# New merge strings for the four step streams of a conv, attention and Fourier kernel

## The chip, the cores and the metric

The kernel runs on one core of a Trainium2 chip. Its metric is the device time of one execution in microseconds. Five engines work side by side, each on its own instructions in order: PE (TensorE, matmuls), DVE (VectorE), ACT (ScalarE), POOL (GpSimd) and SP (SyncE, which here issues all DMAs). They wait for each other on semaphores only.

## What is computed

32 images of 56 x 56 pixels and 24 channels, in f32, go through six residual blocks:

```python
# twice: conditional convolution block, all weights mixed per image
rw = sigmoid(mean(x, (1, 2)) @ Wr + br)                   # 4 experts
h = relu(bn(conv1x1(x, mix(rw, Wpw)) + rw @ bpw))         # 24 -> 96
h = relu(bn(depthwise3x3(h, mix(rw, Wdw)) + ...))
x = x + bn(conv1x1(h, mix(rw, Wpwl)) + rw @ bpwl)         # 96 -> 24
t = tokens(x)                                             # 3136 x 24
t = t + linear_attention(layernorm(t))                    # 6 heads, no softmax
t = t + ffn_fp8(layernorm(t))                             # 24 -> 96 -> 24, rounded to fp8
u = layernorm(t)                                          # Fourier attention over the tokens
X = fft(relu(bn(u @ w1.T)), axis=tokens)
y = real(ifft(relu(X.real * r - X.imag * i + rb) + 1j * relu(X.imag * r + X.real * i + ib)))
t = t + bn(y @ w2.T)
t = t + ffn_fp8(layernorm(t))
```

## The kernel before

The images go in 8 quads of 4. The 4 x 24 channels of a quad lie on partitions, the 3136 tokens on the free axis, in seven chunks of 448. Quads are worked in four streams of steps, and each engine has its own part of each stream:

- c, the convolution's front (`conv_part`): PE's seven input transposes (L698) and ACT's copies of them with a running sum (L1080); DVE's router (`router`, three steps: pooling L1395, logits L1399, mixed weights L1403 to L1421) with PE's logits L708 and ACT's sigmoid L1088; then for each of four slabs of 14 rows PE's hidden 1x1 convolution (L722), ACT's relu (L1099) and the centre tap for two of three channel tiles (L1106), and DVE's other eight taps for these two tiles (L1440, 16 steps a slab, 64 a layer). All of it twice, for two layers.
- d, the convolution's end (`conv_end`): PE's taps of the third tile as diagonal matmuls (L741, 72 in a step), ACT's relus (L1129 of the third tile, L1135 of the two others), PE's output convolution in two halves (L757 and L763), DVE's residual add of each half (L1456). The adds free the bank for the next slab's tensor taps.
- m, the middle: LayerNorm 0, attention, LayerNorm 1, FFN 0. Its first step holds the setup of the late constants (`setup_rest`: ACT L1067 to L1071, three square roots; DVE L1356 to L1384, casts, then a chain behind those roots). A LayerNorm ends with ACT's root (L1155) and DVE's reciprocal of it (L1465), and then seven products, one a chunk (L1482). FFN: PE L903 and L889, ACT L1204, L1195, L1189.
- b, the back: LayerNorm 2, Fourier attention, LayerNorm 3, FFN 1, output transposes (PE L1030, ACT's copies L1280).

The middle stream runs about one quad behind the convolution, the back stream behind the middle. So at most times each engine has steps of three or four streams to choose from, and its order among them is written out by hand: `merged` reads a string of turns for the engine, "c17" for 17 steps of stream c, "m1" for one of m. Once a string has ended, what is left of each stream follows, stream by stream. A step whose input is late holds back everything behind it on its engine.

SP isn't merged. For each quad q it issues the loads of input groups 4 to 6 of q, groups 0 to 3 of q + 1, and the store of q − 2, in that order. The input buffer has four groups; the load of a group waits (`in_tp`) until PE has transposed the group that stood there. The store waits (`ot_ready`) for the last output copy of its quad on ACT. At the start SP loads packs i and k, four groups of input, and packs a, s and b.

The first router of each layer, in the first quad only, also scales the packed weights (`scale_weights`, L1346 to L1351).

Of the kernel before, what the change touches and what calls it, by code (L numbers as in the profile page):

```python
# [84 lines left out]
        "d7 b1 c10 m1 c1 m1 c5 m1 c4 b2 c2 m2 c4 b2 c1 m1 c4 b2 m1 c1 m1 c3 b1 c1 b1 m1 c4 b2 c1 m1 c1 m1 c4 "  # L85
        "b2 c1 m1 c4 b2 m1 c1 m1 c4 b2 c2 m1 c3 b2 c1 m2 c4 b2 m1 c3 b1 c1 b1 m1 c2 m1 c4 b2 c1 m1 c3 b2 m3 "
        "b5 "
    ),
    "tensor": (
# [46 lines left out]
    ),  # L136
    "scalar": (
# [1635 lines left out]
```

How the kernel before makes its waits and increments, by code:

```python
        def hold(eng, signal, value):  # L532
            eng.wait_ge(signal.sem, value)
            stand(eng)
# [35 lines left out]
        @block.sync  # L570
# [1 line left out]
            def load(q, groups):  # L572
                for g in groups:
                    n = q * NCK + g
                    if n >= XG:
                        sp.wait_ge(in_tp.sem, n - XG + 2)
                    o = PAD + RC * BPG * (n % XG)
                    dst = xin[:, o:o + RC * BPG].rearrange("p (j m) -> p j m", j=BPG)
                    for i in range(QI):
                        src = x_v[q * QI + i, :, BPG * CH * g:BPG * CH * (g + 1)].rearrange("p (j c) -> p j c", c=CH)
                        dma = sp.dma_start(dst[:, :, CH * i:CH * (i + 1)], src)
                        dma.then_inc(xin_loaded[n % XG].sem, 16)
# [1 line left out]
            def store(q):  # L585
                sp.wait_ge(ot_ready.sem, ot_ready.at(q, NCK))
                sp.dma_start(out_v[bass.ds(q * QI, QI), :, :].rearrange("b p f -> p b f"), xout).then_inc(out_stored.sem, 16)
# [4 lines left out]
            for key in ("a", "s", "b"):  # L592
                sp.dma_start(pack_t[key], packs[key]).then_inc(par_loaded[key].sem, 16)
            for q in range(NQ):
                load(q, range(XG, NCK))
                if q + 1 < NQ:
                    load(q + 1, range(XG))
                if q >= 2:
                    store(q - 2)
            for q in range(max(NQ - 2, 0), NQ):
                store(q)
            sp.wait_ge(out_stored.sem, 16 * (NQ + 1))
```

## Time and profile before

The median of three runs is 2535.08 us (2534.11 to 2538.29).

| | |
|---|---|
| profiled execution | 2535.46 us, of it the span 2533.7 us |
| busy, share of the span | PE 85%, DVE 76%, ACT 66%, POOL 5% |
| chain that ended last | PE 43%, DVE 35%, ACT 12%, issue 6%, SP's queue 3%, DMA 1% |
| DVE's taps, L1440 | 1024 steps, 989.5 us, 1028 ns each |
| tensor taps, L741 | 4608 matmuls, 404.0 us |
| hidden convolution, L722 | 768 matmuls, 380.7 us |
| DMA | 12 GB/s on the mean |

The share of an engine is its busy time over the span; the chain is followed back from the last instruction, at each step to what released it or to the instruction before it on the engine. No engine is full over the whole span: in the first and the last sixth of it few streams have work.

### The profile page before, as it was taken

How to read it: one execution, taken by the hardware profiler on the slowest of the kernel's cores; microseconds unless marked ns; L12 is line 12 of the kernel's file. 1: busy time of each engine (PE TensorE's matmuls, PEld its weight loads, DVE VectorE, ACT ScalarE, POOL GpSimd, SP SyncE). 2: the span in 40 equal slices, each digit the busy share in tenths (PEclk: the TensorE clock that was granted, in tenths of full speed). 3: DMA queues.
4: the chain of work that ended last, by engine and by line, in shares of the span. 5: the costliest groups of instructions: out<-in, count | busy, mean ns of one | idle time of the engine just before them, and what ended most of it. 6: DMA issues, size and time to landing. Idle time of an engine off the chain costs nothing.

```text
span 2533.7 us, 49146 instructions
## 1 busy us (share of the span) xinstructions
PE 2156.5 (85%) x19776; PEld 1225.0 (48%) x19776; DVE 1916.6 (76%) x3719; ACT 1666.3 (66%) x2822; POOL 116.5 (5%) x290
## 2 busy tenths in 40 slices
PE   3677988999889988999879996899889998987765
PEld 2233433664346633664336633476336643663652
DVE  4975978798968797798948996886977989356153
ACT  3244457866777677766777676775877668867645
POOL 1000000000000000000000000000000000000000
PEclk9887979999989999989889997898999999987866
DMA  5001001000020001100020002000010000000000
GB/s 140 1 1 20 1 1 12 10 2 1 1 39 2 2 1 28 13 2 1 1 39 2 2 1 37 2 2 1 1 27 6 2 1 1 21 1 1 21 1 20
DMA packets 108593, 29.56 MB, mean 12 GB/s; under 512 B 104144, under 2 KB 104272, under 8 KB 107984
## 3 DMA queue, kind: packets, MB, share of 16 engines
q1 hardware_dynamic: 108368, 26.41, 5.1%
q8 instruction: 159, 2.61, 0.4%
q14 instruction: 66, 0.54, 0.1%
HBM read 16.77 MB, written 9.63 MB: 10 GB/s over the span
## 4 chain that ended last, share of the span: by engine, by line
PE 43%; DVE 35%; ACT 12%; issue 6%; SPq 3%; DMA 1%; ACTq 0%; DVEq 0%
DVE acc L1440 17%; PE P L741 8%; PE P L722 6%; PE P L787 5%; PE P L938 4%; SPq L582 3%; PE P L951 3%; DVE SQ L1582 3%; PE P L979 2%; PE P L763 2%; DVE arena L1566 2%; PE P L778 2%; PE P L993 2%; PE P L889 2%; DVE arena L1582 1%
## 5 line engine op out<-in xcount | busy, mean ns | idle before, releaser
L1440 DVE SCALAR_TENSOR_TENSOR acc<-H,Dm,acc 128x784 f32<-128x784 f32 x1024 | 989.5, 1028 | 77.1 <-ACT acc L1106 76.7
L722 PE MATMUL P<-T,Wk 112*128 112x448 f32 (+1 forms) x768 | 380.7, 587 | 55.8 <-DVE biasT L1421 30.7
L741 PE MATMUL P<-H,diag 64*64 64x392 f32 x4608 | 404.0, 500 | 18.3 <-DVE T L1456 18.3
L1099 ACT ACTIVATE H<-P,biasA 128x448 f32<-128x448 f32 (+1 forms) x384 | 236.4, 622 | 131.7 <-PE P L722 109.3
L741 PEld LDWEIGHTS P<-H,diag 64*64 64x64 f32 x4608 | 172.3, 135 | 231.5 <-issue 203.5
L787 PE MATMUL P<-T,pack_b 112*112 112x448 f32 x448 | 227.2, 598 | 23.1 <-DVE T L1541 8.4
L1129 ACT ACTIVATE acc<-P,biasT 128x392 f32<-128x392 f32 x128 | 68.7, 584 | 228.1 <-PE P L741 228.1
L722 PEld LDWEIGHTS P<-T,Wk 112*128 112x128 f32 x768 | 129.4, 198 | 177.2 <-ACT H L1099 80.1
L963 PE MATMUL P<-pack_b,arena 128*96 128x112 f32 x928 | 112.9, 271 | 22.0 <-DVE roots L1582 11.7
L1106 ACT ACTIVATE acc<-H,Dm 128x784 f32<-128x784 f32 x128 | 121.9, 952 | 12.5 <-PE P L763 10.5
L938 PEld LDWEIGHTS P<-pack_b,arena 113*64 113x64 f32 x1792 | 112.7, 215 | 27.5 <-issue 18.9
L963 PEld LDWEIGHTS P<-pack_b,arena 128*96 128x96 f32 x928 | 99.9, 169 | 53.5 <-DVE roots L1582 19.5
L1135 ACT ACTIVATE acc<-acc,biasA 128x784 f32<-128x784 f32 x128 | 120.0, 952 | 7.5 <-DVE acc L1440 7.3
L1456 DVE SCALAR_TENSOR_TENSOR T<-P,bias,T 112x392 f32<-112x392 f32 x128 | 77.3, 621 | 60.5 <-PE P L763 60.0
L938 PE MATMUL P<-pack_b,arena 113*64 113x96 f32 x1792 | 119.9, 292 | 3.2 <-DVE arena L1482 3.2
L1222 ACT ACTIVATE arena<-P 128x384 f32<-128x384 f32 x112 | 94.6, 845 | 32.6 <-PE P L938 26.8
L763 PE MATMUL P<-acc,Wk 128*64 128x392 f32 (+1 forms) x512 | 104.4, 531 | 11.6 <-ACT acc L1135 11.4
L787 PEld LDWEIGHTS P<-T,pack_b 112*112 112x112 f32 x448 | 69.8, 184 | 86.8 <-issue 55.4
L1246 ACT ACTIVATE arena<-P,pack_b 96x224 f32<-96x224 f32 (+1 forms) x128 | 60.0, 518 | 71.6 <-DVE arena L1566 62.6
L1147 ACT ACTIVATE arena<-P 112x448 f32<-112x448 f32 x112 | 60.4, 539 | 64.5 <-PE P L787 62.7
L698 PE MATMUL P<-pack_i,xin 112*112 112x112 f32 x224 | 40.6, 328 | 72.4 <-DMA xin<-in_x 72.4
L951 PEld LDWEIGHTS P<-pack_b,arena 128*64 128x64 f32 x3072 | 91.7, 138 | 16.8 <-issue 10.5
(194 smaller groups left out, 3713.7 us busy)
## 6 DMA issues: line engine op xcount, KB each, us to landing
xin<-in_x SPq DMA_DIRECT2D x224, 42.0 KB, 2.3
out_y<-arena SPq DMA_DIRECT2D x8, 1176.0 KB, 6.0
pack_b<-in_pack_b SPq DMA_DIRECT2D x1, 3820.5 KB, 17.6
arena<-in_pack_s SPq DMA_DIRECT2D x1, 1548.0 KB, 8.8
pack_a<-in_pack_a SPq DMA_DIRECT2D x1, 1084.0 KB, 5.5
pack_i<-in_pack_i SPq DMA_DIRECT2D x1, 320.0 KB, 3.1
arena<-in_pack_k SPq DMA_DIRECT2D x1, 192.0 KB, 3.3
```

Of the source, the lines that this page charges most:

```text
L722: pe.matmul(conv_rows(slice(0, 128), HB[(NP * s + e) % len(HB)], n), Wk1[:, 128 * j:128 * (j + 1)], image_rows(T[q % 3], a, n), start=True ...
L741: last = pe.matmul(conv_rows(slice(64 * h, 64 * (h + 1)), CVB + r, HH), diag[64 * r:64 * (r + 1), tap, :], H1[64 * r:64 * (r + 1), slot(s, ...
L763: last = pe.matmul(conv_rows(out_rows, CVB + h, HH), w, image_rows(acc[:, (NT * s + j) % N2, :], HH * h, HH), start=False, stop=True)
L787: pe.matmul(P[0:R, cen[c % NC], 0:CK], par["cen"][0:R, :], T[q % 3][:, CK * c:CK * (c + 1)], start=True, stop=True).then_inc(norm.cen_psum ...
L938: last = pe.matmul(P[64 * j:64 * (j + 1), FB[g % BN], RC * s:RC * (s + 1)], Y_x[:, 4 * g + s, :], par["fw1"][0:R + 1, RC * j:RC * (j + 1)] ...
L951: last = pe.matmul(P[64 * ri:64 * (ri + 1), FB[g % BN], 2 * K1 * s:2 * K1 * (s + 1)], Hf[:, 8 * g + s, :], par[m][:, :], start=True, stop= ...
L963: last = pe.matmul(P[0:RC, FB[g % BN], o:o + 2 * HW], Y2[:, s // 2, s % 2, :], par["f"][:, s // 2, :], start=True, stop=True)
L1099: act.activation(H1[:, slot(s, j), o:o + n, 1:1 + HW], conv_rows(slice(0, 128), HB[(NP * s + e) % len(HB)], n), ACT.Relu, bias=biasA[:, j, ...
L1106: act.activation(acc[:, (NT * s + j) % N2, :].rearrange("p (r w) -> p r w", w=HW), H1[:, slot(s, j), 1:1 + SR, 1:1 + HW], ACT.Copy, scale= ...
L1135: act.activation(a, a, ACT.Relu, bias=biasA[:, j, 0:1]).then_inc(h2_ready.sem, 1)
L1440: ins = ve.scalar_tensor_tensor(a, H1[:, slot(s, j), r:r + SR, c:c + HW], Dm[:, j, tap:tap + 1], a, ALU.mult, ALU.add)
L1582: last = ve.scalar_tensor_tensor(dst[:, k, 0:n * HW].rearrange("p (s w) -> p s w", w=HW), xi, sc, pp_g[:, k, 0:n * HW].rearrange("p (s w) ...
```

## The change

Only the strings in `TURNS` differ. Each engine runs the same steps, in the same order within a stream, with the same instructions, waits, buffers and banks; the order between the streams is another. PE has 2593 steps, ACT 2273, DVE 2073, POOL 143. The beginning of DVE's string, and the last line of PE's, ACT's and DVE's:

```diff
     "vector": (
-        "m1 c27 d2 c18 d1 c1 d1 c18 d1 c1 d1 c2 d2 c23 d1 c1 d1 c18 d2 c15 d1 c1 d1 c9 d2 m1 c1 m1 c1 m2 c1 "
+        "c3 m1 c21 d2 c17 d2 c14 d2 c12 d2 c23 d2 c20 d2 c14 d2 c10 d2 m1 c1 m2 c1 m2 c1 m3 c17 m1 c2 m1 c2 d1 "
...
     "tensor": (
...
-        "b3 m4 b3 m4 b1 m2 b2 m3 b2 m1 b176 "
+        "m3 b2 m3 b1 m1 b2 m2 b1 m1 b1 m1 b2 m3 b1 m2 b2 m2 b3 m1 b2 m1 b9 m1 b6 m1 b3 m1 b1 m2 b8 m1 b148 "
...
     "scalar": (
...
-        "m2 b1 m18 b1 m5 b2 m5 b2 m2 b3 m1 b155 "
+        "m1 b2 m2 b1 m16 b1 m1 b2 m2 b4 m1 b5 m1 b5 m1 b5 m1 b4 m1 b2 m1 b4 m1 b2 m2 b1 m2 b9 m1 b119 "
...
     "vector": (
...
-        "b2 m2 b2 m1 b2 m1 b2 m2 b2 m2 b2 m2 b2 m1 b7 m1 b7 m8 b1 m2 b3 m2 b3 m1 b1 m4 b1 m3 b2 m1 b78 "
+        "b5 m1 b4 m1 b1 m1 b1 m2 b67 "
```

So on DVE the setup ("m1") stands behind the first router ("c3"). In the first layer of the first quad the pairs of residual adds ("d2") of slabs 0 to 2 stood behind taps 24, 42 and 43, 61 and 62; they now stand behind taps 21, 38 and 52. Read through step by step, the strings also move these:

| place | order before | order now |
|---|---|---|
| start, ACT | setup's roots, first sigmoid | first sigmoid, setup's roots |
| quad 0 to 1, PE | input transposes 3 to 6 ahead of the last variances of LayerNorm 0 | behind them |
| quad 0 to 1, ACT | LayerNorm's root behind input copy 5 | ahead of input copy 2 |
| quad 4 to 5, ACT | last output copy of quad 2 behind the FFN copies of quad 3 | ahead of the FFN copy of chunk 4 |
| quad 4 to 5, PE | input transpose 0 of quad 5 ahead of several FFN matmuls of quad 3 | behind the first of chunk 6 |
| quad 6 to 7, DVE | seven products of LayerNorm 2 ahead of the last residual add | behind it |
| quad 3, end of layer 0 | LayerNorm 3's root on DVE ahead of the last add, PE's output convolution behind that LayerNorm's matmuls | the last add free of the root; PE as before; more LayerNorm and Fourier copies ahead of the relu on ACT |
| tail | FFN 0 of the last quad in the middle stream, then FFN 1 of quad 6 | chunks of both by turns |

## Rows read from the trace of the kernel before

**Rows 1.** Head of the page.
```profile
span 2533.7 us, 49146 instructions
```
**Rows 2.** Windows: stretch, us, busy us (instructions) of PE, PEld, DVE, ACT, POOL; PEclk, DMA.
```profile
0.00:430.00 430.00, 314.87 (x2054) 136.96 (x2056) 329.49 (x542) 195.89 (x327) 18.66 (x43) 0.90 0.10 24
430.00:2160.00 1730.00, 1565.77 (x14770) 895.08 (x14766) 1419.05 (x2739) 1234.85 (x2093) 83.65 (x210) 0.94 0.05 9
```
**Rows 3.** Waits of DVE, 432 to 2160 us: total us, times, longest us.
```profile
DVE acc L1440 <- ACT acc L1106: 54.5, 17, 5.8
DVE T L1456 <- PE P L763: 39.2, 13, 14.0
```
**Rows 4.** Timeline of DVE, 14 to 60: start, us, instruction, [idle before <- releaser].
```profile
19.51 0.57 DVE L1357 CAST selb<-arena 128x784 bf16<-128x784 f32 x1 [5.23 <-DMA arena<-in_pack_s]
...
34.30 0.17 DVE L1368 RECIPROCAL mid<-mid 112x1 f32<-112x1 f32 x1 [12.39 <-ACT arena L1071]
...
39.66 0.56 DVE L1346 TENSOR_TENSOR pack_a<-pack_a,mid 112x384 f32<-112x384 f32 x1
...
54.97 1.03 DVE L1440 SCALAR_TENSOR_TENSOR acc<-H,Dm,acc 128x784 f32<-128x784 f32 x1 [4.86 <-ACT acc L1106]
57.67 2.92 DVE L1440 SCALAR_TENSOR_TENSOR acc<-H,Dm,acc 128x784 f32<-128x784 f32 x3 [1.67 <-ACT acc L1106]
```
**Rows 5.** Timeline of ACT, 12 to 70.
```profile
35.59 1.28 ACT L1088 ACT_TABLE_LOAD   x1
```
**Rows 6.** Waits of DVE, 117 to 150.
```profile
DVE T L1456 <- PE P L763: 11.6, 2, 11.0
```
**Rows 7.** Windows around the last tensor taps of the first layer.
```profile
80.00:99.50 19.50, 10.17 (x92) 4.00 (x92) 19.50 (x26) 8.25 (x14) 0.34 (x2) 0.93 0.00 1
...
118.79:127.60 8.81, 8.75 (x72) 3.27 (x72) 1.83 (x2) 0.00 (x0) 0.00 (x0) 0.70 0.00 0
```
**Rows 8.** Timeline of DVE, 211 to 250, first to second quad.
```profile
215.67 0.62 DVE L1456 SCALAR_TENSOR_TENSOR T<-P,bias,T 112x392 f32<-112x392 f32 x1 [2.53 <-PE P L763]
...
230.04 0.85 DVE L1465 RECIPROCAL mid<-mid 128x112 f32<-128x112 f32 x1 [13.07 <-ACT mid L1155]
...
233.51 0.16 DVE L1395 TENSOR_REDUCE pool<-part 112x1 f32<-112x7 f32 x1
```
**Rows 9.** Timeline of ACT, 217 to 236.
```profile
229.91 0.97 ACT L1080 ACTIVATE T<-P 112x448 f32<-112x448 f32 x1
```
**Rows 10.** Timeline of ACT, 1275 to 1286, fifth to sixth quad.
```profile
1275.96 0.59 ACT L1195 ACTIVATE mid<-P 112x448 f16<-112x448 f32 x1
...
1284.33 0.50 ACT L1280 ACTIVATE arena<-P 112x384 f32<-112x384 f32 x1
```
**Rows 11.** Timeline of SP's issues, 1264 to 1300.
```profile
1271.39 1.91 SPq L582 DMA_DIRECT2D xin<-in_x  x4
1284.86 0.33 SPq L587 DMA_DIRECT2D out_y<-arena  x1
1285.23 15.03 SPq L582 DMA_DIRECT2D xin<-in_x  x22
```
**Rows 12.** Timeline of DVE, 1284 to 1300.
```profile
1297.82 0.16 DVE L1395 TENSOR_REDUCE pool<-part 112x1 f32<-112x7 f32 x1 [12.34 <-ACT T L1080]
```
**Rows 13.** Timeline of PE, 1269 to 1280.
```profile
1270.79 1.33 PE L698 MATMUL P<-pack_i,xin 112*112 112x112 f32 x12
...
1275.88 0.35 PE L903 MATMUL P<-mid,w1q 112*128 112x448 fp8e5 x1
```
**Rows 14.** Timeline of DVE, 1880 to 1910, seventh to eighth quad.
```profile
1884.37 3.27 DVE L1482 TENSOR_TENSOR arena<-arena,P 112x448 f32<-112x448 f32 x6 [3.82 <-PE P L802]
...
1906.00 0.16 DVE L1395 TENSOR_REDUCE pool<-part 112x1 f32<-112x7 f32 x1 [15.87 <-ACT T L1080]
```
**Rows 15.** Timeline of ACT, 2326.5 to 2332, one of five such waits.
```profile
2328.58 0.55 ACT L1195 ACTIVATE arena<-P 112x448 f16<-112x448 f32 x1 [0.65 <-PE P L889]
```
**Rows 16.** Timeline of DVE, 868 to 900, quad 3, end of the first layer.
```profile
881.80 0.62 DVE L1456 SCALAR_TENSOR_TENSOR T<-P,bias,T 112x392 f32<-112x392 f32 x1 [11.44 <-PE P L763]
```

More of the change, by code:

```diff
@@ L84 @@
     "gpsimd": (
-        "d7 b1 c10 m1 c1 m1 c5 m1 c4 b2 c2 m2 c4 b2 c1 m1 c4 b2 m1 c1 m1 c3 b1 c1 b1 m1 c4 b2 c1 m1 c1 m1 c4 "
-        "b2 c1 m1 c4 b2 m1 c1 m1 c4 b2 c2 m1 c3 b2 c1 m2 c4 b2 m1 c3 b1 c1 b1 m1 c2 m1 c4 b2 c1 m1 c3 b2 m3 "
-        "b5 "
[3 rows of a table added]
     ),
     "tensor": (
[46 rows of a table removed]
[48 rows of a table added]
     ),
     "scalar": (
[37 rows of a table removed]
[39 rows of a table added]
     ),
     "vector": (
[23 rows of a table removed]
[28 rows of a table added]
     ),
```

216 rows, old and new, of the table TURNS are left out of this document.

## The prediction

> **What bounds the kernel now.** I read five views, in this order. First the head of the page: the span is 2533.7 us [rows 1]. The profiled execution took 2535.46 us, 1.8 more than its span, and the median of the runs is 2535.08. My sum is made against 2535.5; the 0.4 between that and the median is noise here. Second, the busy time by stretch [rows 2]. From 430 to 2160 us, where all four streams run, PE is busy 1565.77 of 1730 us (90%), DVE 1419.05 (82%), ACT 1234.85 (71%), and the granted clock is 0.94. PE is idle for only 164 us in that stretch, so no order of the same work saves more than that there. Up to 430 us PE is at 73% and DVE at 77%: the pipeline fills, few streams have work, and a wait on DVE is a wait of the kernel. Third, the waits of DVE in the steady stretch [rows 3]: the first taps of a slab wait for the centre tap of ACT (54.5 us over 17 waits), and the residual adds wait for the convolution's output from PE (39.2 us over 13). Fourth and fifth, the chain and the timelines around the places where DVE stands still; they follow with the parts.
>
> No instruction comes or goes with new strings, except where ACT changes between functions. What can change is how long an engine stands at a step whose input is late while ready steps queue behind it. I laid the steps of the new strings, one by one, on the times of the old trace. Start and end of each quad in each stream come out within a few microseconds of the old ones in cumulated busy time, so the large schedule is the same. What remains are local turns; I price the six that stand where DVE or ACT visibly waits, and cost the rest at nothing.
>
> **1. Start: the router ahead of the setup.** On DVE the old order runs the middle stream's setup before the first router. Its casts take 2.4 us (19.51 until 21.91, the end got from 34.30 less 12.39 of idle) and its chain 5.36 (34.30 to 39.66); only then does the router begin [rows 4]. The inputs had been copied by 35.59, where ACT goes on to the sigmoid's table [rows 5]. The new order is router, setup, taps. The router so starts some 4 us earlier and ends at 46.1 in place of 50.1 (54.97 less 4.86 of idle); the setup's 7.7 us follow, until about 53.9. The first tap waited for ACT's centre tap until 54.97, the second, after 1.67 of idle, for the other centre tap until 57.67 [rows 4]; both centre taps are ready by 53.7 when the router is 4 us earlier. The second tap then starts at 54.9 in place of 57.67: **−2.8**. On ACT the setup's square roots go behind the first sigmoid, which adds two table loads of 1.28 us each (the size of the load in [rows 5]). They lie in the 8 us in which DVE computes the router's weights and cost nothing; without that cover they would cost 2.6.
>
> **2. The end of the first convolution layer.** DVE stands 11.0 us for the last convolution output [rows 6]. The tensor taps of the last slab began only at 118.79 and kept PE busy for 8.75 us [rows 7], because the residual adds that free their bank stood behind tap 61 of 64. They now stand behind tap 52, nine or ten taps of 1.03 us [rows 4] earlier: the group then ends at 118.79 − 9.7 + 8.8 = 117.9, before DVE's last tap. What stays is the way from the last tap through ACT and PE, 2.53 us at the second layer of the same quad, where the adds stand earlier [rows 8]: 11.0 − 2.5 = **−8.5**. If PE came only two taps earlier and not nine, the group would end at 125.5 and 2.1 us would come of it; nine is taken since the adds' place is plain in the string.
>
> **3. First to second quad.** DVE waits 13.07 us for ACT's root of the first LayerNorm and does it at 230.04; the router of the next quad follows at 233.51 [rows 8]. The last input copy on ACT had begun at 229.91 and taken 0.97 [rows 9]. In the new order the variance's matmuls stand ahead of the input transposes 3 to 6, and the root ahead of five input copies; DVE's root work falls into the wait for input, and the router starts right behind the last copy, at 230.9: **−2.6**.
>
> **4. Fifth to sixth quad.** SyncE's store of quad 2 waits for that quad's last output copy, which ACT does at 1284.33, behind an FFN copy of 1275.96 [rows 10]; the store goes at 1284.86 and the loads of quad 5's groups 4 to 6 behind it at 1285.23 [rows 11]. DVE's router waits 12.34 us for that input, until 1297.82 [rows 12]. The new order has the output copy ahead of the FFN copy of 1275.96. Against that, PE's input transposes of quad 5 move from 1270.79 to behind the FFN matmul of 1275.88 [rows 13], so group 3's load, issued at 1271.39 over 1.91 us [rows 11], waits until about 1277 and the store until 1278.9. That is 6.3 us earlier than 1285.2: **−6.3**. Lower end 0 (the 5 us of the later transposes comes on top on PE), upper end the whole 12.34; I take 6.3 because both moves have rows.
>
> **5. Seventh to eighth quad.** Six LayerNorm products of 3.27 us in all stand on DVE at 1884.37, and one more of 0.62 behind, ahead of the last residual add; then DVE idles 15.87 us until the next router at 1906.00 [rows 14]. In the new order the add comes first, which lets PE and ACT go on to the input, and the seven products fill the idle time: 7 × 0.615 = **−4.3**.
>
> **6. Tail.** Before the last quad's back part, the seventh quad's FFN 1 runs alone, and in each of its chunks ACT waits 0.65 us for PE, from 2328.58 on, five times [rows 15]: 3.3 us. The new strings interleave these chunks with those of the last quad's FFN 0 (the closing run of back steps alone falls from 176 to 148 on PE, from 155 to 119 on ACT, from 78 to 67 on DVE): **−3.3**.
>
> **What I cost at nothing.** Between the layers of all quads, 15 places, the DVE work of other streams in front of the first taps grows from 48 to 71 us in sum. It lies mostly in the wait for the centre tap (4.86 at the first such place in [rows 4], 5.8 at the worst in the steady stretch by [rows 3]); about 12 us stick out beyond it. They cost 12 if DVE's convolution is the bound there; with PE at 90% I count 0, and keep 12 for the range. At quad 3 DVE waits 11.44 us at 881.80 for PE [rows 16]; PE is busy all through, so the new place of the add behind another step saves or costs about nothing; ends −11 and +14.
>
> Sum: −2.8 − 8.5 − 2.6 − 6.3 − 4.3 − 3.3 = −27.8, so 2535.5 − 27.8 = 2507.7; against the median 2507. **Forecast 2507 us.**
>
> **Rivals.**
>
> A, the likeliest, is this sum with the rest even; its own range is 2495 to 2525 (half of terms 4 and 5 missing, or 12 more gained).
>
> B: the steady stretch gains as well, because the order removes small waits everywhere. For it: 39.2 and 54.5 us of DVE waits [rows 3] and 164 us of idle PE are there to be had. Against: the displacements are small and of both signs. If an eighth of PE's idle time goes, 20 us more: 2488, range 2470 to 2495.
>
> C: nothing. Terms 1, 2 and 6 sum to 14.6 us and come, but terms 3 to 5 don't, since PE at 90% takes back later what an earlier router gives, and the filler's 12 us count against them: 2535.5 − 14.6 + 12 = 2533, range 2525 to 2545. For it: PE's share in [rows 2].
>
> D, the other side: the waits at the ends of layers double. In the steady stretch the adds wait 39.2 us for PE's output [rows 3]. The new strings put more of the LayerNorm and Fourier copies ahead of the convolution's second relu on ACT, and at quad 3 leave PE's second output behind the LayerNorm's matmuls, the place that already costs 11.44 us [rows 16]. If each such wait becomes twice as long, 39 us come on top, while terms 4 and 5, which pass through the same stretch, don't come: 2535.5 − 17.2 + 39 = 2557, range 2540 to 2580. It decides once the waits grow by more than 17 us. Against it: elsewhere the new order moves adds forward (term 2).
>
> E, the clock: in the steady stretch it is granted at 0.94 [rows 2], that is 12% of the time at 1.2 instead of 2.4 GHz. At 0.92 it would be 16%, 4% of 1730 us or 69 us more at half speed, of which half is lost, at 90% busy 31 us. With the sum that gives 2507.7 + 31 = 2539. For it: after the wait at the first layer's end the tap group ran at 0.70, where it had been 0.93 before [rows 7], so each new wait on PE can cost its group speed too. Against: PE has little idle time in the steady stretch, and the new strings are not seen to add any. The Trainium skill (TensorE: Matmul & The Clock Gate, section "HAM oscillation — how this bites in real kernels") says that waits between bursts of matmuls make each burst begin slow again; the trace agrees, with that 0.70 behind the wait.
>
> **How the numbers follow.** A 0.47, B 0.17, C 0.13, D 0.19, E 0.04. Within 0.2%, about 5 us, a measurement can't tell the two kernels apart. Faster are A and B: 0.64. Most of C and E and the low edge of D are the same: 0.16. The rest of D and a little of C are slower: 0.20. The range goes from 2482 (leaving out 0.06 of B) to 2550 (leaving out 0.13 of D).
>
> **What would show it.** Right: in the trace after, DVE's first router near 36 us and its second tap near 55; no wait over 4 us at the first layer's end; routers of quads 5 and 7 waiting under 7 and under 13 us; adds in the steady stretch waiting about 39 us. Wrong: the layer-end waits well above 50 us (D), the clock below 0.93 (E), or the six places better and the time the same (C).

## The result and the profile after

The kernel with the new strings takes 2446.69 us (median of four, 2443.8 to 2447.62) against 2534.6 before: a ratio of 0.966 [0.963, 0.969], 88 us faster. The forecast was 2507, 28 us faster, with 2482 as the lower end of its range. The direction was right, the size off by a factor of three.

I read the profile after in the order of the prediction. First the head of the page, with span and busy time of each engine.

```profile
span 2441.8 us, 49148 instructions
...
PE 2109.1 (86%) x19776; PEld 1203.2 (49%) x19776; DVE 1926.5 (79%) x3719; ACT 1667.9 (68%) x2824; POOL 114.3 (5%) x290
...
DVE 43%; PE 32%; ACT 13%; issue 7%; SPq 3%; DMA 1%; ACTq 0%; DVEq 0%
```

The busy line of the page before, for comparison:

```profile
PE 2156.5 (85%) x19776; PEld 1225.0 (48%) x19776; DVE 1916.6 (76%) x3719; ACT 1666.3 (66%) x2822; POOL 116.5 (5%) x290
```

The span is 91.9 us shorter than in [rows 1]. DVE does the same work in 9.9 us more (1916.6 before), so its idle time fell by 101.8 us, from 617.1 to 515.3. PE does its 19776 matmuls in 47.4 us less (2156.5 before). The chain was 43% PE and 35% DVE before and is 43% DVE and 32% PE now. Two instructions are new, the two table loads on ACT that the prediction counted.

The steady part comes out if one sets windows on the same work: from 20 us behind quad 1's last tap to the last tap of all, which is 448 to 2152 us before and 426 to 2074 after (14671 matmul records in either). The windows view of the kernel before, then of the kernel after, with columns as in [rows 2]:

```profile
448.00:2152.00 1704.00, 1547.24 (x14671) 886.08 (x14669) 1404.83 (x2702) 1215.62 (x2056) 81.01 (x203) 0.94 0.04 8
```

```profile
426.00:2074.00 1648.00, 1512.66 (x14671) 868.91 (x14671) 1417.50 (x2704) 1216.93 (x2061) 78.65 (x201) 0.97 0.05 9
```

This stretch fell by 56 us, the head before it by 22 and the tail behind it by 14. In it DVE's idle time fell from 299.2 to 230.5 us. PE's busy time fell by 34.6 and its idle time by 21.4; the granted clock rose from 0.94 to 0.97. The waits of DVE in this stretch, after, which answer to [rows 3]:

```profile
DVE T L1465 <- PE P L772: 27.6, 11, 7.0
...
DVE T L1533 <- PE P L872: 23.9, 7, 7.0
DVE acc L1449 <- ACT acc L1115: 20.5, 9, 6.9
```

The first taps (lines are nine higher now, L1449 is L1440 of before) wait 20.5 us for the centre tap where they waited 54.5, the residual adds 27.6 where they waited 39.2. Against that, the attention's adds now wait 23.9 us for PE; the same wait before:

```profile
DVE T L1524 <- PE P L863: 7.2, 10, 1.8
```

Where does it come from? I measured for each of the 15 layer ends with a layer behind them how long after the layer's last tap DVE began the first of the last slab's two residual adds (h = 0). This delay holds DVE's work for other streams as well as its waits. Nine of the delays took over 6 us before, one takes that after.

| end of | quad 0 L0 | 2 L0 | 3 L0 | 4 L0 | 6 L0 | 6 L1 | other nine | sum |
|---|---|---|---|---|---|---|---|---|
| before, us | 11.0 | 9.1 | 25.8 | 10.5 | 14.0 | 15.3 | 38.8 | 124.5 |
| after, us | 2.7 | 2.8 | 7.0 | 2.5 | 4.2 | 4.8 | 25.9 | 49.9 |

From the last tap to the first tap of the next layer the 15 places took 514.6 us in sum before and take 456.7 after, with about as much work of other streams on DVE in them (140 and 145 us).

The largest delay is the place of [rows 16]. In the timeline of PE the output convolution of that slab has two parts, the first L757 (L766 after) and the second L763 (L772 after), with LayerNorm's matmuls (L787 and L778, or L796 and L787 after) in between. Before:

```profile
868.52 0.54 PE L757 MATMUL P<-acc,Wk 64*64 64x392 f32 x1
...
880.57 0.38 PE L778 MATMUL P<-SQ,pack_b 112*32 112x112 f32 x8
880.87 1.53 PE L763 MATMUL P<-acc,Wk 128*64 128x392 f32 x8
```

After:

```profile
841.86 0.54 PE L766 MATMUL P<-acc,Wk 64*64 64x392 f32 x1
...
851.51 1.01 PE L796 MATMUL P<-T,pack_b 112*112 112x448 f32 x2
852.44 1.53 PE L772 MATMUL P<-acc,Wk 128*64 128x392 f32 x8
```

The add on DVE, after, which answers to [rows 16]:

```profile
853.37 0.63 DVE L1465 SCALAR_TENSOR_TENSOR T<-P,bias,T 112x392 f32<-112x392 f32 x1 [7.00 <-PE P L772]
```

And PE's windows from DVE's last tap to its add, before and then after:

```profile
856.00:882.00 26.00, 26.00 (x204) 14.84 (x202) 11.44 (x16) 15.36 (x31) 0.00 (x0) 1.00 0.01 1
```

```profile
846.20:853.30 7.10, 6.97 (x49) 2.55 (x50) 0.17 (x1) 6.91 (x14) 0.00 (x0) 1.00 0.00 0
```

PE is full in both, all 26.00 of 26 us before. The second part (L763) also needs ACT's relus of the two other tiles. Before, both had ended by 857.63:

```profile
855.84 1.79 ACT L1135 ACTIVATE acc<-acc,biasA 128x784 f32<-128x784 f32 x2
```

So PE did other ready work for 23 us while this part had its input from ACT. After, the second relu ends at 851.74 and L772 begins at 852.44:

```profile
850.81 0.93 ACT L1144 ACTIVATE acc<-acc,biasA 128x784 f32<-128x784 f32 x1
```

But PE's own order is nearly the same at this place; the second part stands some 34 LayerNorm matmul records further forward. What moved most is DVE's order. Fourteen adds of the attention (L1524) and the Fourier block (L1596), 11.4 us, stood behind the layer's last tap, which ended at 856.04; now they stand ahead of its last three taps. The Fourier adds before, then the same adds and these three taps after:

```profile
862.40 6.78 DVE L1596 SCALAR_TENSOR_TENSOR T<-P,fbias,T 112x448 f32<-112x448 f32 x7
```

```profile
835.57 6.79 DVE L1605 SCALAR_TENSOR_TENSOR T<-P,fbias,T 112x448 f32<-112x448 f32 x7
...
843.45 2.92 DVE L1449 SCALAR_TENSOR_TENSOR acc<-H,Dm,acc 128x784 f32<-128x784 f32 x3
```

So of the 18.8 us by which this delay shrank, about 11 are work that moved ahead of it. DVE's idle time in the two windows fell by 7.6 us, from 14.6 to 6.9.

### The profile page after: what moved, and what is told of

Same layout as the page of the kernel before. It is cut to its first block, busy times and chain, and to the rows that moved or that the text cites. A ratio compares the mean times of both kernels' runs of the same rounds, so it can differ in the third digit from the quotient of the medians.

```text
span 2441.8 us, 49148 instructions
## 1 busy us (share of the span) xinstructions
PE 2109.1 (86%) x19776; PEld 1203.2 (49%) x19776; DVE 1926.5 (79%) x3719; ACT 1667.9 (68%) x2824; POOL 114.3 (5%) x290
## 4 chain that ended last, share of the span: by engine, by line
DVE 43%; PE 32%; ACT 13%; issue 7%; SPq 3%; DMA 1%; ACTq 0%; DVEq 0%
DVE acc L1449 21%; PE P L731 5%; PE P L947 4%; PE P L750 4%; PE P L796 4%; DVE SQ L1591 3%; SPq L591 3%; DVE arena L1575 3%; PE P L960 2%; DVE arena L1591 2%; DVE roots L1591 2%; DVE T L1465 2%; PE P L772 1%; PE P L898 1%; DVE T L1605 1%
## 5 line engine op out<-in xcount | busy, mean ns | idle before, releaser
L1449 DVE SCALAR_TENSOR_TENSOR acc<-H,Dm,acc 128x784 f32<-128x784 f32 x1024 | 997.3, 1030 | 35.9 <-ACT acc L1115 35.3
L731 PE MATMUL P<-T,Wk 112*128 112x448 f32 (+1 forms) x768 | 373.3, 576 | 38.0 <-ACT H L1108 19.2
L750 PE MATMUL P<-H,diag 64*64 64x392 f32 x4608 | 396.4, 493 | 8.3 <-DVE T L1465 5.7
L796 PE MATMUL P<-T,pack_b 112*112 112x448 f32 x448 | 220.7, 584 | 14.5 <-DVE T L1605 3.5
L772 PE MATMUL P<-acc,Wk 128*64 128x392 f32 (+1 forms) x512 | 104.5, 531 | 19.0 <-ACT acc L1144 18.4
L972 PEld LDWEIGHTS P<-pack_b,arena 128*96 128x96 f32 x928 | 100.3, 167 | 33.0 <-issue 14.6
L796 PEld LDWEIGHTS P<-T,pack_b 112*112 112x112 f32 x448 | 69.1, 182 | 72.6 <-issue 47.4
L1213 ACT ACTIVATE arena<-P 128x448 f16<-128x448 f32 x168 | 89.3, 554 | 15.2 <-PE P L912 15.2
L1213 ACT ACTIVATE mid<-P 128x448 f16<-128x448 f32 x168 | 94.4, 565 | 7.7 <-PE P L912 7.3
L707 PE MATMUL P<-pack_i,xin 112*112 112x112 f32 x224 | 42.1, 331 | 66.4 <-DMA xin<-in_x 66.0
```

Of the source, the lines that this page charges most:

```text
L731: pe.matmul(conv_rows(slice(0, 128), HB[(NP * s + e) % len(HB)], n), Wk1[:, 128 * j:128 * (j + 1)], image_rows(T[q % 3], a, n), start=True ...
L750: last = pe.matmul(conv_rows(slice(64 * h, 64 * (h + 1)), CVB + r, HH), diag[64 * r:64 * (r + 1), tap, :], H1[64 * r:64 * (r + 1), slot(s, ...
L772: last = pe.matmul(conv_rows(out_rows, CVB + h, HH), w, image_rows(acc[:, (NT * s + j) % N2, :], HH * h, HH), start=False, stop=True)
L796: pe.matmul(P[0:R, cen[c % NC], 0:CK], par["cen"][0:R, :], T[q % 3][:, CK * c:CK * (c + 1)], start=True, stop=True).then_inc(norm.cen_psum ...
L972: last = pe.matmul(P[0:RC, FB[g % BN], o:o + 2 * HW], Y2[:, s // 2, s % 2, :], par["f"][:, s // 2, :], start=True, stop=True)
L1213: act.activation(f.a[:, c % 2, CK * j:CK * (j + 1)], P[:, hb[v % N1B], 0:CK], ACT.Copy).then_inc(f.half.sem, 1)
```

## The experiments

The first six and the last six reorder turns only; e7 to e10 add instructions to steps of the back stream. The excerpts are from the strings; "|" marks a seam. The time of a kernel is its median, the ratio is to the kernel before on the same chip.

**e1 and e2: the convolution's end alone.** The beginning of DVE's string, e1 against the kernel before, then e2 against the kernel after:

```diff
-m1 c27 d2 c18 d1 c1 d1 c18 d1 c1 d1 c2 d2 c23
+m1 c24 d2 c17 d2 c14 d2 c12 d2 c23
...
-c3 m1 c21 d2 c17 d2 c14
+c3 m1 c32 d2 c16 d2 c13
```

> The kernel before with one part of the change: on every engine the steps of the convolution's end (stream d) stand where the new strings have them relative to the convolution's front (stream c); middle and back stay where the old strings have them relative to c. Theory 1 (the waits at the ends of layers were the loss, and the place of the d steps sets them): most of the 88 us comes, 2534.6 - 60 = about 2475, 2465 to 2490. Theory 2 (the new interleaving of middle and back, that is which filler stands where, is what gains): 2515 to 2530. The prediction's own terms give only the 8.5 us of term 2 and part of term 5: about 2523.

> The mirror image: the kernel after with the d steps put back to where the old strings had them relative to c, middle and back as in the new strings. Theory 1: the gain goes, 2500 to 2515. Theory 2: it stays, 2455 to 2470.

Measured: e1 2820.42 us, 1.112 [1.109, 1.115], and e2 2770.13 us, 1.092 [1.088, 1.095]. Neither theory's range was met, nor that of the prediction's own terms. In e1 the delay at the end of quad 0's first layer fell from 11.0 to 2.7 us as in term 2, but from quad 2 on every layer, counted from last tap to last tap, grew by 9 to 38 us.

The strings are not the clean halves that the expectations describe. In e1, 7 of DVE's 128 adds, 32 of ACT's 256 steps of stream d and 22 of PE's 192 stand up to 6 front steps later than in the new order. In e2, 40 of DVE's 128 adds stand up to 12 taps later than in the old one: the first slab's behind tap 32, where the old order has them behind 24. So e1 shows that nearly the new place of these steps, without the order around it, costs some 285 us. How much of e2's loss comes from the late adds is open.

**e3 and e4: the head alone, the tail alone.** DVE's string at the seams:

```diff
 e3
+c2 m2 d2 c4 m1 c5 | d2 b8 c31 ...
 e4
+m2 b1 c8 m2 c3 | m5 d2 m2 b8 m8 b9 ...
```

> The new order up to the end of the second quad's convolution (406 us in the trace after), then the rest in the old order. The trace after shows the convolution of quad 1 done 20 us earlier. Theory 1 and 2 alike expect it kept to the end: 2534.6 - 20 = 2514, 2509 to 2520. Rival C of the prediction (PE at 90% takes back later what the head gives) expects 2525 to 2534.

> The old order until the last convolution ends (2151 us in the trace before), then the new order for what is left. By the two traces the stretch from there to the end falls by 14 us: 2520, 2516 to 2524. By the prediction's term 6 it falls by 3.3: 2531. If the 14 us were prepared earlier (by which steps are left over when the convolution ends), little of it comes: 2528 to 2534.

Measured: e3 2518.87 us, 0.993 [0.990, 0.996], 18 us of the 20; e4 2529.01 us, 0.998 [0.996, 0.999], 6 us where the trace showed 14 and term 6 said 3.3. What the head gives is kept to the end, against rival C. In e4's trace the tail is 7 us shorter, where it is 14 shorter in the trace after. The other half of the tail's gain so hangs on the order ahead of it, by which steps are left over.

**e5 and e6: late steps of the layer ends moved forward.** PE's string at the end of quad 4's and quad 6's first layer in e5:

```diff
-m1 d1 b13 d1 b3
+m1 d1 b1 d1 b4 d1 b8 d1 b3
...
-m1 b12 d1 b7
+m1 b2 d1 b17
```

> The kernel before, with 77 turns moved forward and nothing else: at the end of each convolution layer (last residual adds of slab 2, and taps, relus, output convolution and adds of slab 3) each step that started later in the trace before than its last input allowed stands where its input is ready. No step of the front, middle or back is moved against another of them. Theory 1a (single convolution-end steps stood late in the old strings, at 7 of 15 layer ends, and that was most of the loss): the ends come 66 us earlier in sum by the trace, PE's other work takes a third of it back: 2490, 2475 to 2505. Theory 2 (the gain is the interleaving as a whole and no small set of steps carries it): 2525 or slower.

> The same edit on the kernel after, by its own trace (75 turns moved forward). The trace after shows the last adds within 7 us of the last tap everywhere, so theory 1a leaves at most some 10 us in it: 2435 to 2450. If moving conv-end steps forward at the cost of the middle and back always pays, 2425 or below; if it costs the other streams more, 2455 or above.

Measured: e5 2614.64 us, 1.031 [1.025, 1.036], 80 us slower than before; e6 2493.16 us, 0.982 [0.977, 0.988], 47 slower than after. Theory 1a fell. The adds did wait less: the delays at the 15 layer ends came to 85.2 us in e5's trace, where they were 124.5. The waits over the whole span, DVE's adds and PE's output convolution for ACT's relu, before and then in e5 (lines are twenty higher there):

```profile
DVE T L1456 <- PE P L763: 60.0, 19, 14.0
...
PE P L757 <- ACT acc L1129: 6.1, 6, 1.9
```

```profile
DVE T L1476 <- PE P L783: 42.1, 19, 7.2
...
PE P L777 <- ACT acc L1149: 30.4, 13, 4.9
```

The adds wait 42.1 us where they waited 60.0, but PE now stands 30.4 us for ACT's relu where it stood 6.1: the output convolution heads its queue before its input is there, and everything behind it waits. That is one visible part of the 80 us; the rest isn't broken down.

**e7 to e10: what an engine's time is worth.** On the kernel after (e7, e8) and before (e9, e10), PE or DVE gets more work in the spectrum steps of the back stream:

```diff
 e7, e9
-                    for s in range(4 * g, min(4 * g + 4, 2 * K1)):
+                    for s in (1 + g % 2) * list(range(4 * g, min(4 * g + 4, 2 * K1))):
 e8, e10
-                    for dst, k, sc in ((m13_g, 0, fneg[:, 1:2]), (m13_g, 1, rd),
+                    for n_, (dst, k, sc) in enumerate(((m13_g, 0, fneg[:, 1:2]), (m13_g, 0, fneg[:, 1:2]), (m13_g, 1, rd),
...
-                        if dst is m13_g and k == 1:
+                        if n_ in (0, 2):
```

> The kernel after with more work for PE: the spectrum matmuls of every odd group are issued twice, 448 records of 0.118 us, 53 us of PE in the back stream. If PE is what binds the steady part, 40 to 55 us longer: 2487 to 2502. If DVE's chain binds it, under 20: below 2467.

> The kernel after with more work for DVE at the same place: the first of the four spectrum products is done twice in each of 120 steps, 52 us of DVE and some 0.1 us of waiting each. If DVE's chain binds the steady part, 45 to 65 us longer: 2492 to 2512. If PE does, under 20: below 2467.

> The kernel before with the extra spectrum matmuls of e7 (39 us of PE busy there, 20 us of time). The prediction took PE, at 90%, for the bound of the steady part: then 30 to 45 us longer than before. If the old strings are bound as the new ones are, by waits on DVE first and by PE for a half, some 20: 2550 to 2560.

> The kernel before with the extra spectrum product of e8 (52 us of DVE busy there, 58 us of time). The prediction, with PE as the bound and 18% of DVE idle, expects under 15 us: below 2550. If every us on DVE counts in the old strings too: 45 to 65 us, 2580 to 2600.

The busy line of the page of each, e7, e8, e9, e10 in this order:

```profile
PE 2148.2 (87%) x20224; PEld 1246.7 (51%) x20224; DVE 1929.1 (78%) x3719; ACT 1670.5 (68%) x2824; POOL 114.2 (5%) x290
```

```profile
PE 2125.0 (85%) x19776; PEld 1212.3 (48%) x19776; DVE 1978.8 (79%) x3839; ACT 1669.4 (67%) x2824; POOL 114.3 (5%) x290
```

```profile
PE 2187.2 (86%) x20224; PEld 1262.6 (49%) x20224; DVE 1922.9 (75%) x3719; ACT 1666.8 (65%) x2822; POOL 114.7 (4%) x290
```

```profile
PE 2167.1 (84%) x19776; PEld 1225.9 (47%) x19776; DVE 1973.6 (76%) x3839; ACT 1667.3 (64%) x2822; POOL 114.7 (4%) x290
```

| whole run | more busy, us | time, us | ratio to before | longer, us | per us of work |
|---|---|---|---|---|---|
| e7, after, PE | 39.1 | 2466.46 | 0.972 [0.965, 0.978] | 15 to 20 | 0.4 to 0.5 |
| e8, after, DVE | 52.3 | 2504.92 | 0.987 [0.981, 0.993] | 54 to 58 | 1.0 to 1.1 |
| e9, before, PE | 30.7 | 2552.14 | 1.007 [1.004, 1.009] | 14 to 17 | 0.5 |
| e10, before, DVE | 57.0 | 2588.24 | 1.022 [1.017, 1.026] | 50 to 55 | 0.9 to 1.0 |

"Longer" is taken from the ratios and from the medians. Part of the added work lies in the tail, where little but the back stream is left: e8 and e10 are 17 us longer there for 13 and 14 us of DVE, e7 and e9 only 3.5 us longer for 9 to 11 us of PE. The steady part alone goes from quad 1's last tap to the last tap of all. Its windows, before, e9, e10:

```profile
428.00:2151.80 1723.80, 1561.82 (x14765) 893.80 (x14764) 1414.40 (x2727) 1229.02 (x2082) 83.65 (x210) 0.94 0.05 9
```

```profile
423.70:2166.20 1742.50, 1585.34 (x15101) 922.31 (x15100) 1419.90 (x2726) 1229.60 (x2083) 82.28 (x210) 0.94 0.05 9
```

```profile
421.20:2187.40 1766.20, 1573.34 (x14764) 894.44 (x14764) 1457.42 (x2817) 1229.82 (x2082) 82.28 (x210) 0.94 0.05 9
```

And after, e7, e8:

```profile
406.50:2074.00 1667.50, 1528.72 (x14772) 876.46 (x14771) 1426.45 (x2730) 1230.45 (x2088) 81.64 (x210) 0.97 0.05 9
```

```profile
406.60:2094.60 1688.00, 1555.94 (x15108) 908.59 (x15107) 1428.73 (x2730) 1232.51 (x2089) 81.62 (x210) 0.97 0.05 9
```

```profile
406.00:2118.00 1712.00, 1536.60 (x14772) 882.01 (x14771) 1465.76 (x2820) 1231.26 (x2088) 81.65 (x210) 0.97 0.05 9
```

| steady part | more busy, us | longer, us | per us of work |
|---|---|---|---|
| e7, after, PE | 27.2 | 20.5 | 0.75 |
| e8, after, DVE | 39.3 | 44.5 | 1.1 |
| e9, before, PE | 23.5 | 18.7 | 0.8 |
| e10, before, DVE | 43.0 | 42.4 | 1.0 |

These are single traces. Ahead of quad 1's last tap, where nothing was added, e9 and e10 already differ from before by 4 and 7 us, so a figure of the steady part can be off by that much.

The spectrum products and matmuls lie on the back stream's chain, so part of what DVE and PE pay there may be that chain's length and not the engine's load; these runs don't separate the two. What is plain is that a microsecond on DVE counts about in full in both kernels, though its share is the lower one. One on PE counts for half over the whole run and for about three quarters in the steady part, so PE isn't slack either.

**e11 and e12: the order changed half-way.** DVE's string at the seam:

```diff
 e11
+b1 c2 b1 m1 c1 b1 m1 c2 b1 m1 b1 c2 | m3 d2 m7 c3 b1 c1 b3 ...
 e12
+c3 m2 b2 c2 m2 c1 b1 c2 | m2 d1 m2 d1 m5 c3 b8 m1 ...
```

> The new order up to the end of the fifth quad's convolution (1223 us in the trace after), then the old. If the gain is made where it is seen and kept, the trace's 41 to 43 us come: 2492 to 2496, and with a seam that costs as that of the head did (2 us) up to 2500. If the steady part's gain hangs on what follows (the order as a whole), less than the head's 18 us is left: 2516 or above.

> The old order up to the end of the fifth quad's convolution (1266 us in the trace before), then the new. If the gain is local, what e11 leaves: 88 - 42 = 46 us, 2488 to 2495. If it hangs on the order as a whole, 2510 or above.

Measured: e11 2499.35 us, 0.987 [0.983, 0.990], 34 to 39 us faster; e12 2486.06 us, 0.981 [0.978, 0.984], 48 to 52 us. Together 82 to 91, against the 88 of the whole change: in time the gain adds up, each half keeps its own.

**e13 and e14: idle gaps filled.** PE's string near the beginning, e13 against the kernel after, e14 against the kernel before:

```diff
-c2 d1 c2 d1 c5
+c2 d1 c7 d1 c3
...
-m1 c3 m2 c3 m2 c1 m1 c1
+m1 c3 m3 c1 m1 c3 m1 c1
```

> The kernel after, with 206 steps (72 on PE, 93 on ACT, 41 on DVE, 153 us of work in all) pulled forward into gaps of the same engine in its trace, each only where its inputs were there and it fits into the gap. Theory a (a stall with ready work behind it is what an order loses by): faster, 2415 to 2440. Theory b (those steps are held so that a more urgent one is not delayed, here or on another engine): no gain or slower, 2440 to 2480.

> The same edit on the kernel before, by its own trace: only 57 steps (23 on PE, 24 on ACT, 10 on DVE, 39 us of work) have their inputs and fit. Theory a: a good part of the 88 us comes, 2490 to 2520. Theory b: next to nothing, 2528 to 2545, since the old strings left hardly any ready step standing.

Measured: e14 2536.87 us, 1.000 [0.999, 1.002]: nothing. e13 2453.7 us, 0.967 [0.965, 0.970], 7 us above the kernel after, whose own ratio of 0.966 its interval holds: nothing, or a little slower. Both runs meet the prediction's premise head on. A count from the traces' semaphore times and the waits in the code shows why e14 had little to fill. In the steady part DVE stood still 268 us before in 76 gaps of over 0.6 us, and in none of them did another stream's next step have all its inputs. After, DVE stands 192 us in 72 such gaps, and in 31 of them a ready step of another stream stands behind for 48 us in sum; on ACT this was 29 us before and is 106 after. So the new strings leave more ready steps standing and still lose less time, and filling the gaps brings nothing. Theory b stands against theory a, though "held on purpose" is not shown, as e13's slowing is within the uncertainty.

**e15 and e16: around the largest wait.** DVE's string at the seams:

```diff
 e15
+d1 c1 b1 m1 b1 c1 m1 b2 c1 b1 c1 b1 m1 c1 | b4 m1 d2 b2 m1 c1 b3 c15 ...
 e16
+b4 m1 b1 m2 c1 m2 b1 m2 c1 | b1 m1 b2 c8 b1 c2 b1 c2 m1 c5 ...
```

> The new order up to the end of the third slab of quad 3's first layer (802 us in the trace after), then the old. By the two traces the convolution is 18 us ahead when quad 3 begins and gives up to 10 of them back within its first layer, in which 8 us more of middle and back work is done. If what a stretch shows is what it is worth, 2516 to 2526; if the 10 us were an investment that pays at the next layer end in either order, 2505 to 2513.

> The new order up to the second tap of quad 3's second layer (878 us in the trace after), then the old. The trace shows it 27 us ahead there: 2505 to 2511 if that is kept. If the wait of 25.8 us that shrinks to 7.0 is a gain of its own, this is some 19 us below e15; if it is only moved work, under 8 below it.

Measured: e15 2517.16 us, 0.992 [0.990, 0.995], and e16 2506.98 us, 0.988 [0.985, 0.991], 10 us below it. Both lie in the ranges for a gain that is worth what the traces show up to the cut. The "wait of 25.8 us" of the expectation is the delay in the table above, of which DVE stood still for 14.6. The 10 us are neither 19 nor under 8, and the two intervals overlap a little, so this is no sharp number. But the traces agree with it: the first layer of quad 3 takes 10.1 us longer after (8 us more of other streams' work is done in it), the transition behind it 18.9 us less, 8.8 net. What is gained at this place is about half of what the delay shrank by, since the other half is work that moved ahead of it.

## Why the prediction was too small

**The bound.** The step that failed is "cost the rest at nothing" for the stretch from 430 to 2160 us, with its reason "with PE at 90% I count 0". The runs show 56 us there, and e10 shows the reason wrong: with PE at 90%, 43 us more of DVE in the kernel before cost 42. So the time of DVE, or of the chain through it, is not covered by PE's load. The prediction had the main place in hand. It read that the other streams' DVE work in front of the first taps grows from 48 to 71 us, mostly within the wait for the centre tap, and put that at 0, or at a cost of 12. The work did grow (45.5 to 69.2 us in the traces, from the router's end to the first tap), and the wait fell from 54.5 to 20.5 us, half of the 68.7 us by which DVE's idle time fell in this part. At the place of [rows 16] it wrote "PE is busy all through, so the new place … saves or costs about nothing"; some 9 us came there by the traces, 10 by e15 and e16.

The sentence that PE's 164 us of idle time are all that an order can save has a gap of its own: it holds PE's busy time fixed. Of the 56 us only 21.4 are idle time of PE; 34.6 are busy time, of the same matmuls at a granted clock of 0.97 in place of 0.94.

**What was looked for.** "What can change is how long an engine stands at a step whose input is late while ready steps queue behind it." On DVE no gap of the steady part was of this kind in the kernel before, and filling what gaps the three engines had brought nothing (e14). What the new strings change in the steady part is which of several ready steps an engine does first. At quad 3, DVE does the adds of other streams ahead of its last taps, so that its wait for PE behind them is shorter, with PE full in both orders.

**The six terms,** as the trace after has them. The second tap starts at 54.5 where 54.9 was forecast, and the setup runs behind the router as worked out. DVE's timeline after, which answers to [rows 4]:

```profile
37.28 0.16 DVE L1404 TENSOR_REDUCE pool<-part 112x1 f32<-112x7 f32 x1
...
53.57 6.71 DVE L1449 SCALAR_TENSOR_TENSOR acc<-H,Dm,acc 128x784 f32<-128x784 f32 x7
```

The first layer's last wait is 2.7 us where 2.5 was forecast. DVE's waits there, which answer to [rows 6]:

```profile
DVE T L1465 <- PE P L772: 3.3, 2, 2.7
```

First to second quad: from the last tap to the next layer's first tap 3.8 us less (2.6 forecast). DVE's timeline, as [rows 8]:

```profile
212.20 0.85 DVE L1474 RECIPROCAL mid<-mid 128x112 f32<-128x112 f32 x1 [6.05 <-ACT mid L1164]
...
219.47 0.16 DVE L1404 TENSOR_REDUCE pool<-part 112x1 f32<-112x7 f32 x1 [3.70 <-ACT T L1089]
```

Fifth to sixth quad: SP's loads follow the convolution's end (1223) by 13 us, where they followed it (1266) by 19, and DVE's router waits 5.71 us instead of the 12.34 of [rows 12]: the 6.3 were right at this place. SP's issues, as [rows 11], and DVE's timeline:

```profile
1235.59 0.49 SPq L596 DMA_DIRECT2D out_y<-arena  x1
1236.12 15.88 SPq L591 DMA_DIRECT2D xin<-in_x  x24
```

```profile
1249.22 0.16 DVE L1404 TENSOR_REDUCE pool<-part 112x1 f32<-112x7 f32 x1 [5.71 <-ACT T L1089]
```

But 20 us of other streams' work now stand on DVE in that transition (12 before), and its length stayed at 53 us; the layer behind it, with less of that work left, took 11.9 us less. Whether the one pays for the other isn't separated. Seventh to eighth quad: 7.5 us less (4.3 forecast, though the row's own 3.27 and 0.62 make 3.9); the router comes 22 us after the last tap where it came after 32. The row that answers to the last of [rows 14]:

```profile
1831.85 0.16 DVE L1404 TENSOR_REDUCE pool<-part 112x1 f32<-112x7 f32 x1 [1.38 <-ACT T L1089]
```

Tail: 14 us by the traces, 6 by e4 (3.3 forecast). So five of the terms came, rather more than less, and of the fourth the wait. They sum to some 40 us in the traces; the other half of the gain lay in places costed at nothing.

**The rivals.** B had the right sign and the reason nearest to it. Its 20 us of PE's idle time came (21.4); what it lacked are the 34.6 us of PE's busy time. C is out by e3 and e11: nothing that the head gives is taken back. D expected the layer ends to wait longer; they wait less at most places, the one at quad 3 included. E expected a lower clock; it rose, from 0.94 to 0.97. At the 0.75 to 0.8 that e7 and e9 give for a microsecond of PE in the steady part, the 34.6 us are an estimated 26 to 28 of the 56. In the other direction the traces of e1 and e5, with the same matmuls, show it too: in their steady part PE idles 343 and 216 us, against 162 before, at a granted clock of 0.90 and 0.92, and is busy 86 and 32 us longer. The windows of e1, then of e5:

```profile
437.00:2428.00 1991.00, 1647.67 (x14763) 919.24 (x14759) 1426.20 (x2725) 1234.78 (x2079) 81.71 (x210) 0.90 0.04 8
```

```profile
417.00:2227.00 1810.00, 1593.94 (x14761) 904.57 (x14760) 1419.36 (x2728) 1230.86 (x2083) 82.30 (x210) 0.92 0.05 8
```

In these orders less idle time of PE went with a faster clock. Whether the clock rose because PE waits less in the new order, or in part for another reason, no run separates; that stays open.

**Open** too: which single choices among the ready steps make the steady part's gain. Both attempts to carry over a part of the order by kind of step (e1, e2) lost over 230 us, with adds that stand partly later than in either order; moving single steps to where their input is ready lost 80 and 47 (e5, e6). Only cuts in time carried over.

## What to carry to other kernels

The busiest engine isn't the bound by its share: add a known amount of work to each engine and see what it costs, stretch by stretch, before pricing any wait at nothing. In an order written out for several in-order engines, look not only for stalls with ready work behind them. Look also for a full engine that does ready work while another one stands and waits for something else from it, and for work of the waiting engine that could go ahead of what it waits behind. Here the order could be cut in time and mixed; mixed by kind of step, it lost.

## What the runs showed that was not expected

Putting conv-end steps exactly where their inputs were ready in the last trace made the kernel before 80 us slower, for 77 turns moved. A step at the head of a queue whose input is late holds back everything behind it; PE stood 30.4 us for one such wait, where it had stood 6.1. The two mixtures by kind of step, e1 and e2, cost 230 to 290 us over the kernel before, about three times what the whole change brings.
